# The last group of a Mamba-2 mixer: chunk products ahead of the preceding output product, and small work on VectorE moved

## The reference

```python
x = x + mixer(layernorm(x))    # in_proj, causal conv, selective scan, gate, norm, out_proj
x = x + swiglu(layernorm(x))   # 4-bit weights: (q - zero) * scale, looked up by group
x = x + attention_over_heads(layernorm(x))
x = x + base_and_lora(layernorm(x))

# the mixer, per head h of 64 (8 groups g of 8 heads), token t:
xBC   = silu(conv4(in_proj(x)))              # x, B, C
state = state * exp(dt*A) + dt*x (outer) B   # 64 x 128
y     = state . C + x * D
yn    = y * rsqrt(mean over the group's 512 channels of y*y + eps) * norm_weight
out   = out_proj(yn * silu(gate))
```

## Time and profile before

| | us |
|---|---|
| median of 3 runs | 1359.0 (1357.73 to 1361.2) |
| the profiled execution | 1357.26 |
| its span | 1355.5 |
| TensorE busy | 1267.2 (93%) |
| VectorE, ScalarE, GpSimd busy | 922.0, 676.6, 550.4 |
| last group with the first feed-forward products, 904.2 to 1041.66 | 137.46, of which TensorE is busy 121.04 |

### The profile page before, as it was taken

One profiled execution on the slowest core, in us unless ns is written; L12 is line 12 of the kernel. 1 busy time (PEld: TensorE's weight loads), 2 busy tenths in 40 slices (PEclk: granted clock), 3 DMA queues, 4 the chain that ended last, 5 costly groups with the idle time before them and its releaser, 6 DMA issues. The chain is left out here.

```text
span 1355.5 us, 20763 instructions
## 1 busy us (share of the span) xinstructions
PE 1267.2 (93%) x6252; PEld 1002.5 (74%) x6262; DVE 922.0 (68%) x1763; ACT 676.6 (50%) x1055; POOL 550.4 (41%) x557
## 2 busy tenths in 40 slices
PE   5699999999999999999999999999988999879986
PEld 3577877777778788778778778877766777667764
DVE  5876666667666766766676676667767555469995
ACT  2466566556655655665566566565453333222220
POOL 3135336433633543453344345433443444343330
PEclk9799999999999999999999999999998999999996
DMA  4211012011001200100120020010012322131200
GB/s 153 59 48 33 1 33 64 18 32 48 24 9 32 63 17 25 55 19 14 32 63 17 2 78 16 17 36 2 6 35 89 96 95 89 55 95 30 59 16 23
DMA packets 44150, 57.61 MB, mean 43 GB/s; under 512 B 10102, under 2 KB 21054, under 8 KB 43824
## 3 DMA queue, kind: packets, MB, share of 16 engines
q1 hardware_dynamic: 44080, 56.85, 13.9%
HBM read 49.87 MB, written 6.96 MB: 42 GB/s over the span
## 5 line engine op out<-in xcount | busy, mean ns | idle before, releaser
L414 POOL TENSOR_TENSOR x_w<-xs,head_g 128x512 f32<-128x512 f32 x56 | 58.6, 1047 | 280.0 <-ACT xs L523 255.5
L616 DVE SCALAR_TENSOR_TENSOR conv<-p_tile,conv_taps,conv 128x511 f32<-128x511 f32 x189 | 140.9, 746 | 28.5 <-ACT conv L490 17.8
L433 POOL TENSOR_TENSOR y<-y,x_d 128x512 f32<-128x512 f32 x56 | 72.0, 1286 | 169.0 <-DVE y L758 169.0
L730 DVE TENSOR_TENSOR em<-em,p_gb 128x512 f32<-128x512 f32 x128 | 82.2, 684 | 73.0 <-ACT em L529 73.0
L495 ACT ACTIVATE xbc<-conv 128x512 f32<-128x512 f32 x96 | 60.6, 631 | 134.2 <-DVE conv L624 77.7
L1030 PEld LDWEIGHTS p_y<-x_dt,em 128*128 128x128 f32 x896 | 108.7, 192 | 16.5 <-issue 13.4
L616 DVE SCALAR_TENSOR_TENSOR conv<-p_d,conv_taps,conv 128x511 f32<-128x511 f32 (+2 forms) x99 | 73.9, 747 | 68.8 <-ACT conv L490 64.9
L94 PE MATMUL p_tile<-xn_hi,wc_hi 128*128 128x512 f32 x252 | 111.3, 442 | 2.8 <-DVE halo L620 2.8
L94 PE MATMUL p_gate<-wr_hi,xn_hi 128*128 128x512 f32 x256 | 106.9, 418 | 1.1 <-ACT gate L511 1.1
L1030 PE MATMUL p_y<-x_dt,em 128*128 128x64 f32 x896 | 106.2, 272 | 1.3 <-DVE x_res L644 1.3
L551 ACT ACTIVATE junk<-y 128x512 f32<-128x512 f32 x64 | 40.5, 633 | 129.2 <-DVE y L781 115.3
(11 more groups left out here) (336 smaller groups left out, 3268.9 us busy)
## 6 DMA issues: line engine op xcount, KB each, us to landing
w_raw<-w SPq DMA_DIRECT2D x112, 256.0 KB, 2.8
q_words<-q SPq DMA_DIRECT2D x33, 256.0 KB, 2.6
h_ring<-h_lo_rows SPq DMA_DIRECT2D x6, 704.0 KB, 4.8
h_lo_rows<-h_rest SPq DMA_DIRECT2D x11, 256.0 KB, 2.0
x_res<-x SPq DMA_DIRECT2D x8, 256.0 KB, 4.2
out<-out_t SPq DMA_DIRECT2D x8, 256.0 KB, 2.0
h_lo_rows<-h_rest SPq DMA_DIRECT2D x11, 128.0 KB, 1.9
decay_lhs<-cum_parts SPq DMA_DIRECT2D x64, 6.0 KB
```

What stands on the lines that cost most here:

```text
L414: pool.tensor_tensor(by_head(x_w[:]), by_head(xs[:, c % 2, :]), heads(DTW, c), ALU.mult)\
L433: pool.tensor_tensor(y[:, c % 2, :], y[:, c % 2, :], x_d[:], ALU.add).then_inc(s_txd, 1)
L616: ve.scalar_tensor_tensor(out=conv[:, s, sh:], in0=p[:, 0:HALF - sh], scalar=conv_w[:, bass.ds(g, 1), j, tap], in1=conv[:, s, sh:], op0=AL ...
L730: ve.tensor_tensor(m, m, gm.unsqueeze(1).broadcast_to([P, HG // 2, P]), ALU.mult)\
```

## The change

**All groups.** The four rests of the output weights on VectorE in chunk 0 all stand behind the later tile's taps.

**Last group only.**
- TensorE, chunks 4 to 7: the chunk product stands ahead of the preceding chunk's output product. In chunks 4 to 6 that output product goes to p_d0, the bank of the decay product (`out_bank`), in chunk 7 to p_y. The decay products of chunks 5 to 7 wait for the residual that read p_d0.
- VectorE: the residual of chunks 4 to 7 and the row rests stand behind z, the row statistics too, in all chunks; the row norms stand ahead of em. The one-hots of gate and up and two unpackings (`up.unpack`) stand at the end of chunk 6, the one-hots of down ahead of the last residual. `small_operands` is split: zero bits in chunk 2, group index in chunk 3, both behind z, and the five operations that split the scales in chunk 3 on GpSimd.
- GpSimd: the power of a row's statistics stands at the top of the chunk two later, ahead of state_dec.
- Behind the group: TensorE makes the z transposes ahead of the spread.

The diff, cut to its core:

```diff
--- before.py
+++ after.py
...
@@ -233,2 +233,6 @@
 
+    def out_bank(last, c):
+
+        return p_d0 if last and CH <= c < NC - 1 else p_y
+
     def bank_of(j):
@@ -368,3 +372,5 @@
 
-            sp.wait_ge(s_q_ve, 12)
+            sp.wait_ge(s_q_op, 5)
+            sp.wait_ge(s_q_z, 3)
+            sp.wait_ge(s_q_i, 5)
             for k in range(PART):
@@ -399,2 +405,15 @@
     def gpsimd(pool):
+        def small_operands():
+
+            pool.wait_ge(s_q_in, 16 * 4)
+            pool.tensor_copy(q_parts[0], q_raw).then_inc(s_q_op, 1)
+            pool.wait_ge(s_q_op, 1)
+            pool.tensor_tensor(q_rest, q_raw, q_parts[0], ALU.subtract).then_inc(s_q_op, 1)
+            pool.wait_ge(s_q_op, 2)
+            pool.tensor_copy(q_parts[1], q_rest).then_inc(s_q_op, 1)
+            pool.wait_ge(s_q_op, 3)
+            pool.tensor_tensor(q_rest, q_rest, q_parts[1], ALU.subtract).then_inc(s_q_op, 1)
+            pool.wait_ge(s_q_op, 4)
+            pool.tensor_copy(q_parts[2], q_rest).then_inc(s_q_op, 1)
+
         def group(g, last):
@@ -403,2 +422,4 @@
                 st = g * (NC - 1) + c
+                if last and c > 1:
+                    rstd_of(c - 2)
                 if 0 < c < NC - 1:
@@ -428,2 +449,4 @@
                         w_rest(g + 1, w)
+                if last and c == CH - 1:
+                    small_operands()
                 if c > 0:
@@ -433,4 +456,2 @@
                     pool.tensor_tensor(y[:, c % 2, :], y[:, c % 2, :], x_d[:], ALU.add).then_inc(s_txd, 1)
-                if last and c > 0:
-                    rstd_of(c - 1)
                 if last and c == CH + 1:
@@ -468,2 +489,3 @@
         up.rest(pool, 0, 0, 0)
+        rstd_of(NC - 2)
         norm(LAST, (NC - 1) % 2)
@@ -638,3 +660,3 @@
 
-        def residual(m, c):
+        def residual(m, c, p):
 
@@ -643,3 +665,3 @@
             wait(ve, s_res, m)
-            ve.scalar_tensor_tensor(out=x_res[:, c, :], in0=p_y[:], scalar=g_rstd[:, c % 2:c % 2 + 1],
+            ve.scalar_tensor_tensor(out=x_res[:, c, :], in0=p[:], scalar=g_rstd[:, c % 2:c % 2 + 1],
                                     in1=x_res[:, c, :], op0=ALU.mult, op1=ALU.add).then_inc(s_res, 1)
@@ -675,7 +697,6 @@
 
-        def small_operands():
+        def zero_bits():
 
-            ve.wait_ge(s_q_in, 16 * 4)
-            ve.tensor_copy(q_parts[0], q_raw).then_inc(s_q_ve, 1)
             words, one_in_pack = (a.rearrange("p (n i) -> p n i", i=PACK) for a in (q_zero, q_zero4))
+            ve.wait_ge(s_q_in, 16 * 4)
             ve.tensor_tensor(one_in_pack, words, q_shift.unsqueeze(1).broadcast_to([P, (NSC + NSD) // PACK, PACK]),
...
@@ -725,2 +743,4 @@
                     z_rest(n - 1)
+                for k in rows_in(last, c):
+                    row_norm(k)
                 ve.wait_ge(s_gm, 2 * (n + 1))
@@ -731,11 +751,3 @@
                         .then_inc(s_m, 1)
-                if last:
-
-                    if c == 2:
-                        small_operands()
-                    if c == NC - 2:
-                        up.hot_gu(ve)
-                    for k in rows_in(last, c):
-                        row_norm(k)
-                else:
+                if not last:
                     for w in SPLIT_IN.get(c, ()):
@@ -745,8 +757,6 @@
                     tile_taps(*tile, range(2))
-                if not first:
-                    residual(n - 1, (c - 1) % NC)
+                if not first and not (last and c >= CH):
+                    residual(n - 1, (c - 1) % NC, p_y)
                 for tile in now:
                     tile_taps(*tile, range(2, TAPPED[tile[3]]))
-                if last and c > 0:
-                    row_stats(c - 1)
                 if c > 0:
@@ -770,9 +780,4 @@
                     tile_taps(*tile, range(1))
-                if c == 0:
-                    w_rest(g, TILES + KT)
-                    w_rest(g, TILES + KT + 1)
-                for k in rows_in(last, c):
-                    row_rest(k)
                 if last and c == NC - 1:
-                    up.dequant(ve, 0, 0, 0)
+                    up.scale(ve, 0, 0, 0)
                 ve.wait_ge(s_intra, n + 1)
@@ -790,2 +795,16 @@
                 ve.tensor_tensor(z[:], y[:, c % 2, :], gate[:], ALU.mult).then_inc(s_z, 1)
+                if last and c >= CH:
+                    residual(n - 1, c - 1, out_bank(last, c))
+                for k in rows_in(last, c):
+                    row_rest(k)
+                if last and c == 2:
+                    zero_bits()
+                if last and c == CH - 1:
+                    group_index()
+                if last and c > 0:
+                    row_stats(c - 1)
+                if last and c == NC - 2:
+                    up.hot_gu(ve)
+                    up.unpack(ve, 0, 0)
+                    up.unpack(ve, 0, 1)
                 for tile in later:
@@ -793,4 +812,4 @@
                 if c == 0:
-                    w_rest(g, TILES + KT + 2)
-                    w_rest(g, TILES + KT + 3)
+                    for k in range(GW // P):
+                        w_rest(g, TILES + KT + k)
 
@@ -889,5 +908,6 @@
         z_rest(LAST)
-        up.dequant(ve, 0, 1, 1)
+        up.scale(ve, 0, 1, 1)
         row_rest(NC - 2)
-        residual(LAST, NC - 1)
+        up.hot_down(ve)
+        residual(LAST, NC - 1, p_y)
         row_stats(NC - 1)
@@ -949,6 +969,6 @@
 
-        def out_product(m):
+        def out_product(m, p):
             wait(pe, s_res, m)
             pe.wait_ge(s_zhi, m + 1)
-            three_pass(pe, p_y[:], lambda k: (zt_hi[:, k, :], zt_lo[:, k, :]),
+            three_pass(pe, p[:], lambda k: (zt_hi[:, k, :], zt_lo[:, k, :]),
                        lambda k: (hi_of(TILES + KT + k), lo_of(TILES + KT + k)), GW // P,
@@ -960,2 +980,3 @@
                 first = isinstance(g, int) and n == 0
+                tail = last and c >= CH
                 left, now, later = conv_tiles(g, last, c)
@@ -987,2 +1008,4 @@
                     pe.wait_ge(l2_lo, k + 1)
+                if tail and c > CH:
+                    pe.wait_ge(s_res, n - 1)
                 for k, p in enumerate((p_d0, p_d1)):
@@ -998,4 +1021,4 @@
                     pe.wait_ge(*lo_count(g, WT - 1))
-                if not first:
-                    out_product(n - 1)
+                if not first and not tail:
+                    out_product(n - 1, p_y)
                 for k in rows_in(last, c):
@@ -1024,6 +1047,8 @@
                 pe.wait_ge(s_xdt, n + 1)
-                if c < NC - 1:
-                    wait(pe, s_res, n)
-                else:
+                if c == NC - 1:
                     pe.wait_ge(s_xs, n + 1)
+                elif tail:
+                    pe.wait_ge(s_res, n - 1)
+                else:
+                    wait(pe, s_res, n)
                 for h in range(HG):
@@ -1032,2 +1057,6 @@
                 mm.then_inc(s_intra, 1)
+                if tail:
+                    if c < NC - 1:
+                        pe.wait_ge(s_e, 2 * (n + 1))
+                    out_product(n - 1, out_bank(last, c))
                 if now:
@@ -1070,2 +1099,3 @@
         group(G - 1, True)
+        z_transpose(LAST)
         pe.wait_ge(s_sg, LAST + 1)
@@ -1073,5 +1103,4 @@
         up.spread(pe, 0, 1, 1)
-        z_transpose(LAST)
         row_transpose(NC - 2, LAST)
-        out_product(LAST)
+        out_product(LAST, p_y)
         up.product(pe, 0, 0, 0)
@@ -1276,3 +1305,3 @@
 
-    def dequant(ve, t, m, slot):
+    def unpack(ve, t, m):
 
@@ -1284,2 +1313,6 @@
                          ALU.bitwise_and).then_inc(s_unp, 1)
+
+    def scale(ve, t, m, slot):
+
+        u = 3 * t + m
         ve.wait_ge(s_dq, u + 1)
...
@@ -1386,4 +1424,5 @@
 
-    up.tables, up.zeros, up.rest, up.round_w, up.dequant, up.hot_gu = tables, zeros, rest, round_w, dequant, hot_of_gu
-    up.spread, up.spread_down, up.product = spread, spread_down, product
...
```

37 lines of the change are left out of this document (20 added, 17 removed).

## The result

The changed kernel takes 1344.21 us (median of 4 runs, 1343.19 to 1348.06), the kernel before 1358.62 in the same comparison. The ratio is 0.9903 with a 95% interval of 0.9889 to 0.9917. The forecast was 1342.0 with 1337 to 1348. The profiled execution took 1348.06 us, the slowest of its four; its span is 1346.2 against 1355.5.

A forecast was written before the change was run, and what follows sets the result against it. TensorE, busy 93% of the span, was taken as the bound, so only its waits count. From 1357.26 us, A -10.2, B -2.7, C -0.9 and D -1.5 sum to -15.3: 1342.0 us, range 1337 to 1348.

The forecast's parts named there:

- A: Chunk 0, all 8 groups: weight rests moved behind the taps shorten the decay product's wait, 1.32 us a group, 10.2 in all.
- the rests end where they ended: Chunk 0 on VectorE: four rests in a row end as two and two did, so weight loads start no later.
- Rival 1: Inner groups: ScalarE's queue delays the exponentials, so each group gives 0.44 us instead of 1.32; 1348 us; chance 12%.
- B: Last group, chunks 1 to 3: +0.9 for later halo taps, residual and z waits removed, table splits free; -2.7 us.
- C: Last group, chunks 4 to 6: reordering removes z and gate waits (-4.6), adds decay waits (+2.2) and norm contention (+1.5); -0.9 us.
- the 1.5 us for row norms: Last group, chunks 4 to 6: row norms overlapping GpSimd operations cost 0.7 each in chunks 4 and 5; bounds 0 and 3.
- D: Chunk 7 and feed-forward start: -3.7 us despite a 4.2 us hole, +3.8 and -1.6 for clock; -1.5 us.
- the first slow stretch: Chunk 7: one spell of TensorE at the 1.2 GHz level behind the 4.2 us hole, costing 1.9 us.
- the -1.6 at the end: Feed-forward start: no low-clock spell after the last wait, where the kernel before lost 1.6 us.
- Rival 3: Chunk 7: hole or short waits bring no low-clock spell, gaining 1.9 to 3.8 us more; 1338 to 1340 us; chance 12%.
- Rival 2: Last group, chunks 4 to 7: VectorE's single file makes the reordered tail cost +2 us; 1346 us; chance 14%.
- rival 4: Last group: GpSimd's power waits in a ring through VectorE and TensorE over a whole chunk; slower, 1368 us; chance 3%.

## Why the prediction held, and where its terms did not

**A, weight rests: mechanism right, size wrong.** Forecast 1.32 us a group, measured 119.92 - 119.01 = 0.91, and 0.95 in the last as forecast. The step that failed is "the rests end where they ended". The order was weighed for the queue of VectorE alone. Moved later, the fourth rest lies beside GpSimd's x_w and x_dt, so that the four take 3.52 us and not 2.8, and the output product, whose position had moved up with everything else, now meets them: 799.50 where TensorE was free at about 799.14 (the row ahead starts at 798.23 and has four matmuls of 0.23). The waits say 0.36 start to start; with GpSimd held back the group gains the full 1.34. Rival 1 named the right place and the wrong engine: ScalarE's exponentials began at 799.50 and no instruction of TensorE waited for them. Cost of the error: 9.2 - 6.5 = 2.7 us in seven groups (1.04 in the first, 0.91 in six).

**B, chunks 1 to 3: right.** The new decay wait is 0.74 printed (forecast 0.9 with signalling), the residual and z waits are gone. From the start of chunk 2 to that of chunk 5, where B ends, 42.40 us became 39.50: -2.90 against -2.7. The five table splits took 2.0 us on GpSimd between 950.75 and 952.77 and ended 1.85 us before its y addition: hidden, as costed.

**C, chunks 4 to 6: the balance right, a term too high.** Chunks 5 and 6 gave -1.74 together. The two decay waits of 1.03 are the 1.1 forecast. Of the 1.5 us for row norms beside GpSimd little was paid: the two of chunk 5 took 2.07 us (973.62) in place of 1.00, so the contention of the earlier trace rows is there, but the row transposes wait only 0.25 us for them, since the gate product fills the time. By the Trainium skill (SBUF — State Buffer, section "SBUF: two separate sides") these two engines share a port pair with an exclusive lock: whichever starts first has it for its whole instruction, where VectorE's reads two operands from SBUF or runs in a two-port mode. The rows agree: x_w holds from 797.78 to 798.90 and the fourth rest ends 0.54 us behind it; the norms of chunk 5 lie beside state_dec (973.18, 1.04 us) and x_w (974.18, 1.23 us). But no wait of the chunk product came of it, and the cost of this contention appeared in part A, where I had not looked.

**D, chunk 7: the hole right, the clock wrong.** The hole was forecast at 4.2 us and is 3.7 start to start; chunk 7 to the feed-forward part was to stay at 30.4 us and takes 32.84. The failed term is the first slow stretch, priced at 1.9 us as the mean of the two seen before. It lost 8.4 x 0.5 + 4.3 x 0.1 = 4.6. The second is as forecast (4.7 x 0.14 + 4.0 x 0.26 = 1.7), and the -1.6 at the end came too. I had read two stretches of 6.3 and 4.6 us and taken their length for a property of the chip. It is not: behind a hole of 3.35 to 3.48 us TensorE worked at the lower level for 9 us here, for 12 in two of the experiments with the same waits, and for 3 in the two kernels without the decay waits of 1.03, 1.03 and 0.44 ahead. These waits have a part in it, as far as seven traces can tell; why 9 in one and 12 in another is open. Rival 3, a kinder clock, did not come, for both stretches did; with the hole filled, which it did not name, the first is gone and the kernel takes 1340.20.

In sum, for the profiled execution: A gave 2.7 us less than forecast, D 2.3 less ahead of the second mark, B 0.2 and C 0.8 more. The first mark lies 0.3 later, and the stages behind the second, which were to be 1.6 shorter, take 318.45 us where they took 318.37: the 1.6 us came (VectorE's instructions lie 1.5 earlier up to 147 us behind the mark) and were lost to the clock in the stages that the change leaves alone (granted 0.50 from 1183.9 to 1187.3, where the kernel before had full clock). 1342.0 + 2.7 + 2.3 - 0.2 - 0.8 + 0.3 + 1.7 = 1348.0, beside 1348.06 measured. This accounts for the slowest of the four executions, which itself lies just outside the range. Both medians, 1344.2 and 1346.8, are in it; the others of the four, 1343.2 to 1344.2, had mean clocks of 0.976 to 0.981 where the profiled one had 0.975, and no trace shows where they were faster. That the medians lie nearer to the forecast than this sum is therefore not explained by its terms; part of it may be luck. Rival 2 (the tail gives nothing, 1346) is therefore about half true, for a reason it did not name; rival 4, the ring through GpSimd, has no wait to show.
